# Work reordered around the shared experts of a fused attention and mixture-of-experts kernel

## The reference

```
x = x + xattn(layernorm(x), ctx, ctx)      # x: 2 x 2048 x 512, ctx: 2 x 128 x 512
x = x + ffn(layernorm(x))                  # 4096 tokens

xattn: q = xWq+bq, k = ctxWk+bk, v = ctxWv+bv, padded to 2048
       c = Re(q)Re(k) - i Im(q)Im(k) in the Fourier domain;  corr = irfft(c)
       mean of corr over heads and channels -> the 15 best delays, softmax weights
       out = sum_k weight_k * v shifted by delay_k, then @ Wo + bo
ffn:   shared = (silu(x Wg) * (x Wu)) Wd,  hidden 1024
       router: sigmoid scores of 16 experts, the best 2 of 4 groups, the best 4 experts
       routed = sum over a token's 4 experts of w_e * (silu(x G_e) * (x U_e)) D_e,  hidden 128
```

## Time and profile before

| | us |
|---|---|
| median of 3 runs | 1020.34 (1014.81 to 1022.12) |
| the profiled execution's own time | 1021.87 |
| its span | 1020.1 |
| PE busy | 996.6 (98%) |
| DVE busy | 649.0 (64%) |
| ACT busy | 381.1 (37%) |
| POOL busy | 441.4 (43%) |
| mean granted TensorE clock | 0.988 of full speed |

### The profile page before, as it was taken

The page is one execution under the profiler, slowest core; times in us unless marked ns, Lnnn a source line. Parts: engine busy times, 40 slices in busy tenths (PEclk is TensorE's granted clock), DMA queues, the critical chain, the costliest instruction groups (busy, mean ns, idle before and its releaser), DMA issues.

```text
span 1020.1 us, 21011 instructions
## 1 busy us (share of the span) xinstructions
PE 996.6 (98%) x6754; PEld 610.1 (60%) x6754; DVE 649.0 (64%) x1534; ACT 381.1 (37%) x776; POOL 441.4 (43%) x508
## 2 busy tenths in 40 slices
PE   9999899999999999999999999999999999999997
PEld 7686564444444444445778777787777854444443
DVE  4857747766268688977555555555555536587777
ACT  3626424433354334322444444444444431111111
POOL 0723602131134322214544454544454337777774
PEclk9979979999999999999999999999999999999999
DMA  9644765858936351412899999899888858999786
GB/s 327 237 150 146 276 195 133 238 155 231 264 110 170 135 145 63 128 59 66 241 265 252 270 271 272 252 258 264 239 250 247 229 172 239 297 300 353 239 251 203
DMA packets 177547, 219.02 MB, mean 215 GB/s; under 512 B 101240, under 2 KB 113400, under 8 KB 176440
## 3 DMA queue, kind: packets, MB, share of 16 engines
q1 hardware_dynamic: 153704, 139.05, 46.4%
q0 software_dynamic: 23760, 78.79, 25.7%
HBM read 124.72 MB, written 70.27 MB: 191 GB/s over the span
## 4 chain that ended last, share of the span: by engine, by line
PE 68%; POOL 13%; issue 6%; DVE 5%; DMA 4%; ACT 2%; SPq 1%; POOLq 0%; DVEq 0%; ACTq 0%
PE bank L1055 18%; PE bank L929 16%; POOL arena L2057 13%; PE bank L1079 9%; PE bank L945 8%; PE bank L1038 5%; PE bank L696 2%; PE bank L716 2%; DMA pt_dram<-arena 2%; PE bank L1069 2%; PE bank L783 1%; DMA arena<-pt_dram 1%; PE bank L771 1%; PE bank L961 1%; PE bank L790 1%
## 5 line engine op out<-in xcount | busy, mean ns | idle before, releaser
L929 PE MATMUL bank<-arena 128*128 128x512 f16 x960 | 221.2, 382 | 4.6 <-DMA arena<-pt_dram 4.4
L1055 PE MATMUL bank<-arena 128*128 x1716 | 210.9, 273 | 1.2 <-DVE arena L1610 1.0
L1055 PEld LDWEIGHTS bank<-arena 128*128 128x128 f16 x1716 | 163.1, 98 | 26.6 <-issue 1.8
L2012 POOL DMA_INDIRECT arena<-xr_dram,arena x143 | 140.5, 983 | 59.3 <-issue 48.0
L2057 POOL DMA_INDIRECT arena<-y_dram,arena x128 | 139.0, 1086 | 57.1 <-issue 36.3
L929 PEld LDWEIGHTS bank<-arena 128*128 128x128 f16 x960 | 95.0, 100 | 113.9 <-DMA arena<-pt_dram 5.2
L1116 PE MATMUL bank<-arena 128*128 128x512 f16 x576 | 128.1, 379 | 0.0
L1079 PE MATMUL bank<-arena 128*128 x429 | 115.4, 378 | 0.0
L1323 ACT ACTIVATE arena<-arena 128x512 f16<-128x512 f32 x64 | 40.3, 629 | 196.5 <-DVE arena L1593 110.9
L945 PE MATMUL bank<-arena 128*128 128x512 f16 x480 | 110.5, 380 | 0.6 <-DVE arena L1595 0.6
L1848 DVE SCALAR_TENSOR_TENSOR arena<-bank,arena 128x128 f32<-128x128 f32 x143 | 41.7, 292 | 108.8 <-ACT arena L1375 108.0
(11 more groups left out here) (226 smaller groups left out, 1286.0 us busy)
## 6 DMA issues: line engine op xcount, KB each, us to landing
y_dram<-arena SPq DMA_DIRECT2D x143, 256.0 KB
arena<-in_x SPq DMA_DIRECT2D x8, 1024.0 KB, 12.0
xr_dram<-arena SPq DMA_DIRECT2D x16, 512.0 KB, 4.2
x_dram<-arena SPq DMA_DIRECT2D x8, 1024.0 KB, 6.0
arena<-in_gu_w SPq DMA_DIRECT2D x16, 512.0 KB, 3.5
out<-arena SPq DMA_DIRECT2D x32, 256.0 KB, 4.2
arena<-x_dram SPq DMA_DIRECT2D x5, 1024.0 KB, 6.1
arena<-x1s_dram SPq DMA_DIRECT2D x20, 256.0 KB, 5.1
```

The costliest lines, as they stand in the source:

```text
L929: last = mm(bank[half][:, :], (gu_hi_s, gu_lo_s)[wp][:, c, at:at + H], xt[:, xv * KC + kc, :], start=(n == 0), stop=(n == 3 * KC - 1))
L1055: last = mm(bank[2 + j][:, 0:2 * H], rows[:, xv * KC + kc, :], only((gu_hi_r, gu_lo_r)[wp], e, slice(kc * 2 * H, (kc + 1) * 2 * H)), start ...
L2012: pool.indirect_dma_start(out=dst, out_offset=None, in_=xr_dram[:, :], in_offset=bass.IndirectOffsetOnAxis(ap=token_now[:, r:r + 1], axis= ...
```

## The change

1. The context is loaded whole in one transfer, ahead of `wk`, and not in two halves (the second had its own semaphore, `s_ctx`).
2. `wv` is loaded after `skew_late(0)` on the SP queue, and not between the two parts of `skew_early`.
3. `turn_first(0)` comes ahead of `second_k(3)`. On ACT the first of the saves of block 0 comes ahead of `first_std(1)`.
4. `correlate(7)` comes ahead of the turns of block 0's second parts. On ACT `save_turned(7)` comes ahead of `shared_weights_hi(0)`, and `save_pt(7)` right behind it, ahead of the saves of block 0's turns.
5. POOL waits for the late skew of batch 1 before it loads shared weights 4 and 5.
6. In chunks of `NORM` (3, 5, 7, 9, 11, 13) ACT does `silu(g)` ahead of `second_hi`.
7. On DVE the low parts of weights 5, 6 and 7 move from the ends of chunks 2, 4 and 5 into chunks 3, 5 and 6, behind an `x1_tile`.
8. `places()` comes after `shared_half(22, 1)`.
9. Routed block 0's rows are saved, and its `gate_up(0)` done, ahead of `shared_down(39)`. Routed blocks 0 and 1 use banks 6 and 7 for gate and up. `shared_sum(4)` reads the banks in the order 4, 5, 2, 3 and stands behind `hidden(0)` on DVE.

```diff
@@ -322,7 +322,7 @@
         s_x = [sem(f"x_in{q}") for q in range(NB)]
-        s_misc, s_ctx = sem("router_in"), sem("second_ctx_in")
+        s_misc = sem("router_in")
         s_mm, s_mm_sb = sem("projection_done"), sem("projection_saved")
@@ -398,6 +398,7 @@
         GATE_UP = ((0, 1), (6, 7))
+        BANKS_FREE = (2, 3, 0, 1)
         FIRST_G = (3, 4, 5, 6)
@@ -407,6 +408,10 @@
             return 3 * (s // 4) + s % 4
+
+        def gate_up_bank(s, n):
+
+            return bank[(6 if isinstance(s, int) and s < 2 else 2) + n % 2]
@@ -422,11 +427,10 @@
-            sp.dma_start(ctx_sb[:, :, 0:M], ctxT[:, :, 0:M]).then_inc(s_kw, 16)
+            sp.dma_start(ctx_sb, ctxT).then_inc(s_kw, 16)
             sp.dma_start(wk_sb[:, 0:KC // 2, :], wk[:, 0:KC // 2, :]).then_inc(s_kw, 16)
             sp.dma_start(bias_sb, biases).then_inc(s_kw2, 16)
-            sp.dma_start(ctx_sb[:, :, M:2 * M], ctxT[:, :, M:2 * M]).then_inc(s_ctx, 16)
             x_in(0)
@@ -532,9 +536,9 @@
             skew_early(0)
-            sp.dma_start(wv_sb, wv).then_inc(s_vw, 16)
             skew_early(1)
             skew_late(0)
+            sp.dma_start(wv_sb, wv).then_inc(s_vw, 16)
             x_in(6)
@@ -621,7 +625,7 @@
             def x1s_tile_out(k, t):
-                sp.wait_ge(s_x1s, TB * k + t + 1)
+                sp.wait_ge(s_x1s, TB * k + BANKS_FREE.index(t) + 1)
                 sp.dma_start(x1s_dram[k][:, t, :], x1b[:, t, :]).then_inc(s_x1sw, 16)
@@ -797,7 +801,6 @@
                         last.then_inc(s_mm, 1)
-            pe.wait_ge(s_ctx, 16)
             for c in range(3):
@@ -808,10 +811,10 @@
                 project(bank[FIRST_G[c]][:, 0:M], lambda k: wq_sb[:, k, c * P:c * P + P], lambda k: column(kT, k, 0))
+            pe.wait_ge(s_const, 16)
+            pe.wait_ge(s_mm_sb, 6)
+            turn_first(0)
             second_k(3)
-            pe.wait_ge(s_const, 16)
-            pe.wait_ge(s_mm_sb, 9)
-            turn_first(0)
             turn_first(1)
@@ -888,6 +891,8 @@
             pe.wait_ge(s_rt, 3)
+            pe.wait_ge(s_vo, 2)
+            correlate(7)
             for p, t in enumerate(ORDER):
@@ -895,8 +900,6 @@
                 last.then_inc(s_r0, 1)
-            pe.wait_ge(s_vo, 2)
-            correlate(7)
             pe.wait_ge(s_x1, TB + 1)
@@ -988,11 +991,11 @@
                     next_attention(ATTEND[g - 1], 3)
-                if g == PLACES:
-                    places()
                 if g:
                 shared_half(g, 1)
+                if g == PLACES:
+                    places()
                 if g == 0:
@@ -1049,10 +1052,10 @@
                     pe.wait_ge(s_rh, s - 1)
-                else:
-                    pe.wait_ge(s_x1s, (FIRST - 1) * TB + j + 1)
+                if s in (2, 3):
+                    pe.wait_ge(s_x1s, (FIRST - 1) * TB + s + 1)
                 for n, (xv, wp, kc) in enumerate((xv, wp, kc) for xv, wp in PARTS for kc in range(KC)):
-                    last = mm(bank[2 + j][:, 0:2 * H], rows[:, xv * KC + kc, :],
+                    last = mm(gate_up_bank(s, s)[:, 0:2 * H], rows[:, xv * KC + kc, :],
                               only((gu_hi_r, gu_lo_r)[wp], e, slice(kc * 2 * H, (kc + 1) * 2 * H)),
@@ -1064,7 +1067,7 @@
                 else:
-                    pe.wait_ge(s_x1s, (FIRST - 1) * TB + j + 3)
+                    pe.wait_ge(s_x1s, (FIRST - 1) * TB + j + 1)
                 for v in range(2):
@@ -1086,10 +1089,10 @@
             turn_rows(1)
-            shared_down(FIRST * SH - 1)
             pe.wait_ge(s_expert, 1)
             gate_up(0, of[0])
+            shared_down(FIRST * SH - 1)
             for s in range(BLOCKS + 1):
@@ -1198,8 +1201,9 @@
                 save_columns(g_sb, c, 0, bank[FIRST_G[c]][:, 0:M], None)
+            save_turned(0, (0,))
             first_std(1)
-            save_turned(0, (0, 1))
+            save_turned(0, (1,))
             normalise(1)
@@ -1300,14 +1304,14 @@
             A(vo[:, 1, 0, :], bank[5][:, :], ACT.Copy).then_inc(s_mm_sb, 1)
+            save_turned(7)
             shared_weights_hi(0)
-            save_turned(7)
+            save_pt(7)
             for p in (0, 2):
             shared_weights_hi(1)
-            save_pt(7)
             second_std(1)
@@ -1337,12 +1341,12 @@
                     tile_exp(1)
-                if g in NORM and g:
-                    second_hi(NORM[g], NORM[g] % 2)
                 if g == 0:
                 silu(g)
+                if g in NORM and g:
+                    second_hi(NORM[g], NORM[g] % 2)
                 if g == 0:
@@ -1372,7 +1376,7 @@
                     act.wait_ge(s_rh, s - 1)
-                A(r_silu[:, j, :], bank[2 + j][:, 0:P], ACT.Silu, scale=1.0 / WS).then_inc(s_rs, 1)
+                A(r_silu[:, j, :], gate_up_bank(s, n)[:, 0:P], ACT.Silu, scale=1.0 / WS).then_inc(s_rs, 1)
                 act.wait_ge(s_rh, s + 1)
@@ -1584,6 +1588,14 @@
+            def save_rows(s, n, p):
+
+                j = on_tensor(n) % 2
+                dve.wait_ge(s_tx, p + 1)
+                if not isinstance(s, int) or s >= 4 or n == 2:
+                    dve.wait_ge(s_rg, s - (1 if n % 4 == 2 else 2))
+                V.tensor_copy(xgT[:, j, :, :], bank16[j].rearrange("p (n q) -> p n q", n=2 * KC)).then_inc(s_txe, 1)
+
             def shared_chunk(g):
@@ -1591,6 +1603,8 @@
                 V.scalar_tensor_tensor(s_h, bank[1][:, :], 1.0 / WS, s_silu, ALU.mult, ALU.mult).then_inc(s_sh32, 1)
+                if g == FIRST * SH - 1:
+                    save_rows(0, 0, 0)
                 dve.wait_ge(s_shh, g + 1)
@@ -1602,11 +1616,11 @@
-            def shared_sum(k):
+            def shared_sum(k, order=range(TB)):
                 dve.wait_ge(s_x1i, 16 * (k + 1))
-                for t in range(TB):
+                for t in order:
                     V.scalar_tensor_tensor(x1b[:, t, :], bank[2 + t][:, :], 1.0 / WS, x1b[:, t, :], ALU.mult, ALU.add
@@ -1652,6 +1666,9 @@
                     x1_tile(ATTEND[g], 0, 6)
+                if g in (3, 5):
+                    for n in WEIGHTS[g - 1]:
+                        shared_weights_lo(n)
                 if g - 1 in ROUTE:
@@ -1664,6 +1681,9 @@
                     x1_tile(ATTEND[g - 1], 2, 6)
+                    if g == 6:
+                        for n in WEIGHTS[g - 1]:
+                            shared_weights_lo(n)
                     if g == 2:
@@ -1676,8 +1696,9 @@
                     best_of_all(1)
-                for n in WEIGHTS.get(g, ()):
-                    shared_weights_lo(n)
+                if g == 1:
+                    for n in WEIGHTS[g]:
+                        shared_weights_lo(n)
                 if g % SH == 0 and g:
@@ -1830,14 +1851,6 @@
-            def save_rows(s, n, p):
-
-                j = on_tensor(n) % 2
-                dve.wait_ge(s_tx, p + 1)
-                if not isinstance(s, int) or s >= 4 or n == 2:
-                    dve.wait_ge(s_rg, s - (1 if n % 4 == 2 else 2))
-                V.tensor_copy(xgT[:, j, :, :], bank16[j].rearrange("p (n q) -> p n q", n=2 * KC)).then_inc(s_txe, 1)
-
             def hidden(s, n):
@@ -1845,7 +1858,7 @@
                     dve.wait_ge(s_rhl, s - 1)
-                V.scalar_tensor_tensor(r_h[:, j, :], bank[2 + j][:, H:2 * H], 1.0 / WS, r_silu[:, j, :], ALU.mult, ALU.mult
+                V.scalar_tensor_tensor(r_h[:, j, :], gate_up_bank(s, n)[:, H:2 * H], 1.0 / WS, r_silu[:, j, :], ALU.mult, ALU.mult
                                        ).then_inc(s_rh, 1)
@@ -1859,10 +1872,9 @@
-            for s in range(2):
-                save_rows(s, s, s)
-            shared_sum(FIRST - 1)
+            save_rows(1, 1, 1)
             hidden(0, 0)
+            shared_sum(FIRST - 1, BANKS_FREE)
             for s in range(UNROLLED):
@@ -1977,6 +1989,7 @@
             pool.wait_ge(s_pt, NB)
+            pool.wait_ge(s_sk2[1], 48)
             for n in range(4, 6):
             pool.wait_ge(s_shl, 1)
```

## The result

| | before | after |
|---|---|---|
| median us (lowest to highest) | 1021.23 (1014.81 to 1026.33), 4 runs | 1005.37 (1003.53 to 1006.32), 4 runs |
| the profiled execution | 1021.87, span 1020.1 | 1005.55, span 1003.7 |
| PE busy | 996.6 | 986.9 |
| DVE busy | 649.0 | 661.2 |
| mean granted clock | 0.988 | 0.996 |

The account below looks back on a forecast made before the run. TensorE (PE) was taken as the bound, busy 996.6 of 1020.1 us, leaving only its waits and half-rate time to win. The terms summed to -20.5 from 1021.87, giving 1001.4 us (chance 0.50), with an 8-in-10 range of 997 to 1012.

Parts of the forecast that it names:

- Second wait and second slow stretch: Batch 1's late skew wait in chunk 1 goes, -4.4 us; clock no longer falls in 125 to 150 us, -6.3.
- +0.9: Charge for correlate(7) and its saves first: later shared weight and block 0 saves delay PE before chunk 0, between 0 and 2.
- bound of -1.9: Smallest gain allowed on the 4.4 us wait in chunk 1, if held-back loads free nothing for the reads.
- First slow stretch: Clock in 50 to 75 us no longer falls once no wait precedes it: -5.0 us, between -5.0 and 0.
- Rival (a): First slow stretch stays, as two-column sums alone lower the clock; all the rest holds: 1005.4 us, chance 0.22.
- The row in chunk 0: Evidence against rival (a): sums in chunk 0, with matmuls between, kept a clock of 1.00.
- Turns and context: Turns ahead of second_k(3) remove a 0.6 us wait for a save, -0.6; context in one load, 0.
- wv: wv behind batch 0's late skew: waits of 1.7 us go nearly whole, -1.6; +1.0 charged for wv and x_in(7) late.
- SiLU and conversions: Four waits of 4.2 us for x1_tile in attention shrink: -3.6 us, between -4.2 and -2.
- places(): One half chunk later, 2.6 us of matmuls cover the 0.9 us wait: -0.9, between -0.9 and 0.
- Routed entry: Routed block 0 first fills a 0.56 us hole, but a new one opens behind shared_sum: 0, between -0.6 and +1.5.
- (c): Small stalls only move, with DVE the bound in chunks 2 to 6: 1005.8 us, chance 0.10.

Follow-up runs that it names:

- corr_only: Kernel before with change 4 alone (last correlation of batch 1 ahead of block 0's turns): median 1045.04 us against 1058.38, ratio 0.997 (0.992 to 1.001).
- loads_free: Changed kernel without change 5, POOL's wait for the late skew ahead of shared weights 4 and 5: 1005.15 us.
- neither: Changed kernel with changes 4 and 5 both taken back: 1050.92 us beside 1055.64 of the kernel before.
- corr_late: Changed kernel with change 4 taken back, the last correlation of batch 1 behind block 0's turns again: 1008.31 us.
- the fillers: Changed kernel with matmuls of zeros beside batch 0's sums (also in a second run with further edits): median 1034.76 us, ratio 0.981 to the kernel before.
- entry_mixed: Changed kernel with DVE's bank sums, routed block 2's row copy and hidden(1) interleaved at the routed entry: 1040.1 us.
- silu_late: Changed kernel with second_hi ahead of silu on ACT again, in the chunks of the second normalisation: 1008.0 us.
- wv_early: Changed kernel with change 2 taken back, the load of wv between the two parts of the early skew again: 1040.85 us.
- changed_again: Changed kernel without an edit, run again: median 1039.0 us beside 1058.38 of the kernel before, ratio 0.986 (0.977 to 0.995).

## Why the prediction was right, and where it was off

- **Second wait and second slow stretch** (-4.4, -6.3, and +0.9 charged): right in size, 10.6 us against 9.8. The +0.9 was not paid. The attribution was wrong, and the right size came by another way than mine. I gave 2.5 of the 4.4 us to the held-back weights alone (hence the bound of -1.9); in the stretch of `corr_only` 9.4 of the 10.6 us came without holding back, and `loads_free` lost nothing. Loads issued ahead of the reads go with slow reads: the last landed after 9.4 and 9.8 us with four and three of them ahead (before, `neither`), after 7.3 and 6.1 with one (`corr_only`, `loads_free`), after 4.1 to 5.9 with the loads held back. But I counted all 1.5 MB as if they stood ahead of the reads whatever the write did, and overlooked that reads issued earlier also pass some of the loads.
- **First slow stretch** (-5.0): the step that failed. The clause "with no wait ... a chance of about 7 in 10" took the wait for the cause. Lost to the clock were 5.1 us before and 3.4 after, so 1.7 came, and even this may be luck: `corr_only`, with the first stage of the kernel before, also lost 3.4. Rival (a) had it right that the stretch stays without a wait, as `corr_late` shows. That the two-column sums lower the clock is argued from where it fell; the fillers don't settle it. The row in chunk 0 that I held against it had 512-column matmuls between the sums, and here nothing stands between the last six pairs.
- **Turns and context** (-0.6, 0): PE was 1.1 us ahead at `correlate(0)`, 0.4 of it from the start (and the start moves by itself: the first one-column matmul stood at 14.5 to 16.0 us in the ten traces with this start and no filler). But I did not ask what that meets next. It met the early skew, whose landing came only 0.26 us sooner, and 0.85 went into a longer wait there. The same microsecond can only be won if the next landing moves too.
- **`wv`** (-1.6 + 1.0): the waits of 1.31 and 0.28 us are gone, with 0.4 of gaps around them. The charge of 1.0 was not paid: `value_part(0)` started at 56.36 with no wait. In `loads_free` it waited 0.5 us for `wv` and in `entry_mixed` 0.3, so the margin of 0.4 was as thin as worked out, and that it held in this trace was luck.
- **SiLU and conversions** (-3.6): off by far. The chunk stretch won 1.8 us with `places()` in it. "DVE's total is the same" was the failed step: its busy time grew by 12.2 us, since the low parts that took 1.36 to 1.38 us before took 2.39 to 3.90 now, as they started earlier in POOL's subtraction. PE's waits for attention tiles fell by 1.0 us and not by 3.6. The row of POOL's 4.07 us operation was in the trace before, at 164.93, with the 1.37 us low part at 168.17 ending 0.54 after it. I had not looked at POOL's timeline there.
- **`places()`** (-0.9): 0.3 by the waits; 0.6 moved to the next matmuls that need the vector engine.
- **Routed entry** (0): 9.01 us before and 8.96 after from `turn_rows` to `gate_up(2)`. The first hole only fell from 0.56 to 0.44, and the new one I named (1.40) is there.
- **The sum.** 20.5 forecast, 16.4 measured: 2.5 short in the first stage, 0.8 more in chunk 0, 2.7 short in the chunks, 0.2 more at the end. The likeliest case had half the chance, and what came was (a) together with the idea of (c), small stalls that move, by another engine than (c) named. That the time is (a)'s 1005.4 is luck: (a) has the chunks win 4.5 us, and the 2.7 short there were made up for by 1.5 more than (a) gives in the first stage, with a low stretch that cost 3.4 us and not 5.0, and by the 0.9 not paid in chunk 0.

## What to carry to other kernels

A wait just ahead of a slow-clock stretch need not be its cause; look at what PE does as the clock falls, and don't take a busy PE for a safe clock (in `corr_late` it fell with PE busy for 14.90 of 15 us and no wait for skew). When PE gets ahead, ask at once for the next landing it will meet, and put the gain into the sum only as far as that landing moves. When an instruction of the vector engine is moved in time, see what the general engine runs beside it (here 0.69 us became up to 3.90), and test two remedies for one wait apart from each other before crediting either.

## What the runs showed of the hardware

- The clock fell with PE busy for 12.00 of the 12 us ahead of it (`corr_late`, at two-column float32 sums). In the nine traces of the changed kernel's unedited first stage this cost 3.4 us four times, 5.1 twice, and 13.7 to 15.4 three times.
- A low part of 0.69 us on the vector engine was held to 3.90 us by one subtraction on POOL, and ended 0.54 to 0.56 us after it each time (six cases each in before, after and `silu_late`).
- A load of 1 MB just ahead of a write of 256 KB in the same queue: 6.8 and 8.4 us from the write's issue to its read, against 4.5 without (before, `wv_early`, after).
- Waits of PE of 1.1 us (`corr_only`, chunk 1) left the clock at 1.00, and those of 4.4 and 4.7 us (before, `neither`) were followed by a low clock (0.73 in 125 to 150 us in both).
- In the later runs the kernel before was 34 to 37 us slower and the changed one 34, and PE lost time in the last stage with nothing to wait for. The waits of `changed_again`, and 34 us of its last stage beside the same of after:

```profile
PE bank L1119 <- issue: 9.6, 15, 1.8
...
PE bank L1131 <- DVE arena L1933: 3.8, 1, 3.8
```
```profile
826.00:860.00 34.00, 28.36 (x106) 10.60 (x105) 14.88 (x22) 3.57 (x6) 19.99 (x20) 0.80 0.62 190
```
```profile
826.00:860.00 34.00, 34.00 (x160) 15.38 (x158) 22.98 (x33) 5.38 (x9) 26.68 (x25) 1.00 0.89 268
```

The first row of windows is `changed_again`, the second the changed kernel of the first run. PE stood for 5.6 us there, and the clock was 0.80. "Issue" says that no event of the profile released it. From its first matmul to the end, the last stage took 219.1 us there and 193.6 after. The cause is open, and no run tests one.
